# Moving a gate, a normalisation and a pair of rounded copies between the slots of a software-pipelined attention kernel

## The reference

```python
x = x + _L0_xattn_ref(_layernorm(x), ctx_2048, ...)   # banded attention, 8 heads, band 64
x = x + _L0_ffn_ref(_layernorm(x), ...)               # top half of the rows through a GELU network
x = x + _L1_xattn_ref(_layernorm(x), ctx, ctx, ...)   # grouped attention, 32 heads, 8 groups
x = x + _L1_ffn_ref(_layernorm(x), ...)               # squared-ReLU network, experts, normalisation
```

```python
x = jnp.transpose(mask, (0, 2, 1))            # mask: the normalised input, 64 x 256 for each of 16
qkv = x @ w_in.T + b_in
q, k, v = jnp.split(qkv, 3, axis=-1)          # 8 heads of 8
scores = jnp.einsum('bqhd,bkhd->bhqk', q, k) / jnp.sqrt(d)
scores = jnp.where(band[None, None], scores, neg)          # |q - k| <= 64
attn = jax.nn.softmax(scores, axis=-1)
o = jnp.einsum('bhqk,bkhd->bqhd', attn, v).reshape(n, t, e)
o = jnp.transpose(o @ w_out.T + b_out, (0, 2, 1))
y = jax.nn.relu(o) * encodings
out = jnp.einsum('nit,io->not', y, w_ct) + b_ct[None, :, None]
```

## Time and profile before

| | before |
|---|---|
| median of 3 runs | 334.32 us (333.77 to 334.48) |
| profiled execution | 333.68 us |
| its span | 331.9 us |
| mean granted TensorE clock | 0.997 |
| PE busy | 307.6 us (93%) |
| DVE busy | 238.3 us (72%) |
| ACT busy | 198.5 us (60%) |
| POOL busy | 181.1 us (55%) |

### The profile page before, as it was taken

How to read it: one execution, slowest core, us unless ns; L and a number is a source line. 1 busy time by engine, 2 the same in 40 slices (tenths; PEclk the granted TensorE clock), 3 DMA queues, 4 the chain that set the end, 5 groups by cost and what they waited for, 6 DMA issues and landing times.

```text
span 331.9 us, 7213 instructions
## 1 busy us (share of the span) xinstructions
PE 307.6 (93%) x2178; PEld 240.2 (72%) x2178; DVE 238.3 (72%) x919; ACT 198.5 (60%) x414; POOL 181.1 (55%) x294
## 2 busy tenths in 40 slices
PE   5997989999999999999998998989899999999993
PEld 4976667677777777776587876757677577898892
DVE  7878889999999999984426336875988647651354
ACT  3748987877778778777640424386878844114210
POOL 7738565677695947586613611453454942325522
PEclk9999999999999999999999999999999999999998
DMA  6999010201010110100000000000000000000000
GB/s 189 365 366 355 13 46 5 49 2 43 9 34 15 27 24 20 35 0 4 2 0 0 2 0 0 0 2 3 0 1 2 2 0 0 2 33 17 18 32 32
DMA packets 13301, 14.51 MB, mean 44 GB/s; under 512 B 2512, under 2 KB 11984, under 8 KB 13264
## 3 DMA queue, kind: packets, MB, share of 16 engines
q1 hardware_dynamic: 12688, 13.72, 13.2%
q10 hardware_dynamic: 576, 0.33, 0.3%
HBM read 10.64 MB, written 1.05 MB: 35 GB/s over the span
## 4 chain that ended last, share of the span: by engine, by line
PE 63%; POOL 12%; DVE 12%; issue 8%; ACT 4%; DMA 1%; POOLq 0%; SPq 0%; DVEq 0%; ACTq 0%
PE ST L803 8%; PE S L439 5%; PE O L466 5%; PE S L778 5%; PE ST L450 4%; PE S L573 4%; PE PJ L402 2%; POOL hT L1104 2%; POOL rstd L1088 2%; PE PJ L698 2%; PE S L721 2%; PE S L654 2%; DVE masked L1300 2%; POOL ex L1145 2%; DVE mw L1432 2%
## 5 line engine op out<-in xcount | busy, mean ns | idle before, releaser
L1300 DVE CUSTOM_DVE_ANT_0 masked<-S,band 128x192 bf16<-128x192 f32 x256 | 79.7, 353 | 9.0 <-PE S L439 7.3
L900 ACT ACTIVATE ex<-ST 128x384 f32<-128x384 f32 x128 | 60.8, 490 | 17.6 <-PE ST L450 16.1
L1085 POOL TENSOR_SCALAR rstd<-mv 128x1 f32<-128x1 f32 x40 | 12.0, 301 | 77.2 <-DVE mv L1236 76.9
L439 PE MATMUL S<-qk 128*128 128x384 f32 x128 | 52.2, 409 | 0.8 <-DVE mw L1300 0.4
L450 PE MATMUL ST<-qk 128*128 128x192 f32 x256 | 48.1, 271 | 2.4 <-ACT ex L900 2.0
L450 PEld LDWEIGHTS ST<-qk 128*128 128x128 f32 x256 | 45.0, 189 | 4.8 <-issue 4.2
L1145 POOL TENSOR_SCALAR_AFFINE_SELECT ex<-ex 128x512 f32<-128x512 f32 x32 | 20.3, 636 | 29.7 <-ACT ex L900 29.6
L466 PE MATMUL O<-ex,v 128*32 128x192 f32 x512 | 34.1, 338 | 0.0
L439 PEld LDWEIGHTS S<-qk 128*128 128x128 f32 x128 | 24.1, 189 | 13.3 <-issue 11.7
L869 ACT ACTIVATE hs<-PJ,sb,byhead 128x512 fp32r<-128x512 f32 x29 | 22.6, 778 | 11.1 <-PE PJ L403 10.8
L803 PE MATMUL ST<-down,hT 128*128 128x256 f32 x128 | 28.9, 379 | 0.0
(11 more groups left out here) (205 smaller groups left out, 717.6 us busy)
## 6 DMA issues: line engine op xcount, KB each, us to landing
qk<-kp SPq DMA_DIRECT2D x48, 48.0 KB
w<-in_w SPq DMA_DIRECT2D x2, 1024.0 KB, 10.1
cx<-in_cx SPq DMA_DIRECT2D x1, 1024.0 KB, 9.7
up<-in_up SPq DMA_DIRECT2D x1, 1024.0 KB, 11.7
down<-in_down SPq DMA_DIRECT2D x1, 1024.0 KB, 10.6
out<-x SPq DMA_DIRECT2D x8, 128.0 KB, 1.7
cxT<-in_cxT SPq DMA_DIRECT2D x1, 768.0 KB, 6.7
x<-in_x SPq DMA_DIRECT2D x1, 768.0 KB, 8.5
```

The costliest lines, as they stand in the source:

```text
L439: mm(out, r32(qp[:, t % 2, g, b, P * c:P * c + P]), r32(mv_), start=True, stop=True).then_inc(s["pe_s"], 1)
L900: A(ex[:, (n // 2) % 4, 2 * w:2 * w + 2, :], ST[n % 2][:, 0:2 * WIN].rearrange("p (h k) -> p h k", h=2), ACT.Exp, scale=SCALE).then_inc(s[ ...
L1300: last = V.tensor_tensor_reduce(out=masked[:, n % 2, h, :], in0=S[n % 2][:, WIN * h:WIN * h + WIN], in1=band[:, c, :], scale=1.0, scalar=N ...
```

## The change

The normalisation of tiles 2 to 7 moves from slot 9 to slot 11 on GpSimd, and behind the gate in the source. The gate moves from slot 11 to slot 10, where it stands before that slot's selects. For tiles 2 to 7 ACT's rounded copies move from slot 14 to slot 15, and VectorE's second low part from slot 1 to slot 0, right behind the first. No step is added or removed and no buffer or wait changes.

```diff
-        SLOT = {"stat": -25, "inv": -24, "norm": -23,
+        SLOT = {"stat": -25, "inv": -24, "norm": -21,
...
-                "turn": 39, "turned": 40, "weigh": 41, "relu": 42, "gate": 43, "gated": 45, "add": 46,
+                "turn": 39, "turned": 40, "weigh": 41, "relu": 42, "gate": 42, "gated": 45, "add": 46,
...
                 t = T_ + 2
-                if l == 14 and 0 <= t < TILES:
+                if l == (14 if t < 2 else 15) and 0 <= t < TILES:
                     act.wait_ge(*normalised(t))
...
-                t = due("norm", T_, l)
-                if t and t >= 2:
-                    pool.wait_ge(s["pool_rstd"], t + 1)
-                    pool.wait_ge(s["pe_v"], t - 1)
-                    normalise(xn[:, t % 2, :], t, "pool_xn")
                 t = due("gate", T_, l)
...
                     G.tensor_tensor(yr[:, 1, :], yr[:, 0, :], cx[:, t, :], ALU.mult).then_inc(s["pool_y"], 1)
+                t = due("norm", T_, l)
+                if t and t >= 2:
+                    pool.wait_ge(s["pool_rstd"], t + 1)
+                    pool.wait_ge(s["pe_v"], t - 1)
+                    normalise(xn[:, t % 2, :], t, "pool_xn")
...
-                if l == (2 if T_ < 1 else 1) and 0 <= t < TILES:
+                if l == (2 if T_ < 1 else 0) and 0 <= t < TILES:
                     dve.wait_ge(*rounded(t, 1))
                     V.tensor_tensor(r32(xs[0:64, 1, :]), xn[64:128, t % 2, :], xs[64:128, 1, :], ALU.subtract)\
```

## The result

| | before | after |
|---|---|---|
| median | 334.12 us (333.77 to 335.51, 6 runs) | 331.97 us (331.85 to 332.05, 6 runs) |
| profiled execution, its span | 333.68, 331.9 us | 331.85, 330.1 us |
| mean granted TensorE clock | 0.997 | 0.995 |

The ratio of after to before, run side by side, is 0.9932, with a 95% interval of 0.9916 to 0.9949: 2.2 us faster, 1.7 to 2.8. The forecast was 333.2, or 1.15 us faster, within 331.5 to 334.9.

The account below looks back on a forecast made before the run. VectorE was taken as nearly full (19.48 of 20.00 us), with two paths almost equal. Seams at 31, 48, 65 us and three later: -0.5 + 0.1 + 0 - 3 x 0.25 = -1.15; 334.32 - 1.15 = 333.2 us, range 331.5 to 334.9.

Parts of the forecast that it names:

- The seam's sum: From slot 13 of a tile to slot 3 of the next, VectorE gains 0.63 us if nothing is in the way.
- Gate 0.20: PE's gated product at slot 13 no longer waits for GpSimd's gate; VectorE can use 0.20 us of it.
- gap 0.15: VectorE's gap before the masked add of slot 1 goes, as S of slot 1 is early: 0.15 us.
- break 0.11: Back-to-back low parts leave VectorE three breaks between neighbouring operations instead of four: 0.11 us.
- slot 3 0.17: From the product of L1315 to the next operation VectorE takes 0.76 instead of 0.93 us: 0.17 us gained.
- the collision: In slot 0, VectorE's low parts and GpSimd's selects hold one another up, leaving 0 to 0.5 us of 0.63.
- A tie: First select and first low part both start at 84.24 us; the seam gains 0.51 or nothing, middle 0.25 us taken.
- Tiles 6 and 7 ... 0: These tiles have no copies and their gate already comes in time, so they gain 0.
- The seam at 31 us: PE's 0.60 us wait for the second low part mostly goes and PE carries it through the tile: -0.5 us.
- No collision: Rival: selects of slot 0 come wholly before or after the low parts; -3.0 us, 331.3 us, chance 0.20.
- kept port: Rival: GpSimd keeps the port over both selects of slot 0, delaying the first low part; +0.9, 335.2 us, chance 0.15.
- no effect: Rival: something counted as slack holds VectorE, or the 31 us stall moves elsewhere; within 0.3 us of before, chance 0.15.

Follow-up runs that it names:

- with the collision taken away: The changed kernel with GpSimd's selects of slot 0 at the six seams made to wait for the second low part: 330.0 us, 0.9884 of before.
- the last experiment: The changed kernel with the gates of tiles 4 and 5, which run beside tiles 6 and 7, back in slot 11: 332.36 us, 0.9954 of before.

## Why the prediction was half right

**The seam's sum held.** Gate 0.20, gap 0.15, break 0.11 and slot 3 0.17 made 0.63, and with the collision taken away the seams at 83, 101 and 119 us gave 0.62, 0.63 and 0.64. In that trace, at 83 us, the first low part starts 1.43 us sooner than before, 0.20 of it gained since the seam ahead, the masked adds of slot 1 start 0.04 us behind the end of the pair, and slot 3 takes 0.76 us. Alone, the gate gave 0.24 and the low part 0.27 (0.16 and its 0.11 of collision); the copies gave 0.10 alone and nothing within the whole at these seams, as long as the collision was there.

**"A tie" was none.** I had select and low part both begin at 84.24 us. In the trace the select is first, by 0.16 us, at every full seam. VectorE came 0.20 us sooner, as counted; PE did not come 0.31 sooner but 0.46 (its shift against before grows from -0.73 us at slot 6 to -1.19 at S of slot 14), and ACT and GpSimd with it. Half of that error is the product "without a wait": the one of 133.00 had itself waited, for a gate of the kernel before that ended at 132.95, 0.05 us ahead of it:

```profile
132.21 0.74 POOL L1122 TENSOR_TENSOR yr<-yr,cx 128x256 f32<-128x256 f32 x1
```

A start right behind the end of its input is no undisturbed start, whether or not the view prints a wait. Where the gate was long done, the product follows ST by 0.20 or 0.21 us (79.02, 131.62 and 147.02 us after the change), not 0.28. The other 0.07 us lies behind the product, in a piece that I had taken as unchanged: from its start to S of slot 14 PE takes 0.93 us (79.02 to 79.95) instead of 1.00 (80.14 to 81.14). Nothing on record says why. The other terms then follow by my own rule: with the select 0.16 us ahead the loss is 0.60 - 0.16 = 0.44, and the seam gives 0.63 - 0.44 = 0.19. I had taken the middle, 0.25; three seams give 0.59 instead of 0.75.

The rule of the Trainium skill, "SBUF — State Buffer", section "Who interferes with whom", that a VectorE operation with two SBUF inputs and a GpSimd one that reads SBUF exclude each other, agrees with the trace: when the two meet, the one that came second ends some 0.27 us (the low parts) or 0.50 us (the wide select) behind the end of the other, and the masked adds, which read their scores from PSUM and only the band from SBUF, take 0.35 us during a select.

**"Tiles 6 and 7 ... 0"** is the largest miss: -0.45, of which the last experiment takes 0.44 away. I had looked at slot 13 of tile 6 only, and read there a product that had waited. In tile 7 of the kernel before, the gate began behind two selects, ended at 148.64 us, and the product started right behind it:

```profile
147.91 0.73 POOL L1122 TENSOR_TENSOR yr<-yr,cx 128x256 f32<-128x256 f32 x1
```
```profile
148.70 0.70 PE L496 MATMUL XB<-yr,wc 128*128 128x256 f32 x2
```

The prediction called itself wrong if a gain arose outside the seams. A quarter of the gain did, so that in this it was wrong; the other sign, a period from 70 to 120 us outside 17.3 to 17.85, did not come (17.66). PE's projection without a wait, which it had also announced, holds at 31 us but not later.

**The seam at 31 us: nearly the right size, by luck, with the wrong mechanism.** -0.36 against -0.5. PE's wait for the second low part, which I had priced, is worth nothing by slot 6, since ACT is full there; the copies' move gave all of it (-0.37 alone, and -0.03 for the change without it), through ACT. The step that failed is "PE, which goes on without a gap from there, carries it through the tile": `hs` stands between.

**48 and 65 us:** -0.06 and -0.28 against +0.1 and 0; without the collision -0.43 and -0.65 against "about 0.3 each". The collision itself costs 0.37 at both. At 65 the missing 0.3 is for the most part the gate, which alone gave 0.22 there. At 48 the parts alone, with the low part's 0.11 of collision taken away, gave 0.28 and 0.11, together 0.39 of the 0.43; the prediction gives no terms for its 0.3, so which of them it had too small stays open.

In all: +0.14 at 31, -0.16 at 48, -0.28 at 65, +0.16 at the full seams and -0.45 behind them make -0.59, from -1.15 to -1.74. That errors of 0.30 one way stood against 0.89 the other is luck. That the medians differ by 2.15 us where the profiled executions differ by 1.83 lies within the interval. No collision was priced at -3.0 us and measured at -3.86, of which 0.54 lie behind the seams, where the price had nothing.

**The rivals.** The kept port and no effect are refuted. The collision is there, and it costs the change 1.9 us of span that the wait gives back.

## What to carry to other kernels

Before a step is moved into a slot, look at what the *other* engine of a shared port does there, and at which of them comes first: two gains on two paths of different size shift the tie that was computed for one. If the engine with slack can wait (here about 2 us before a select), one wait that serialises the pair can be cheaper than letting them meet: here it was worth 0.43 us at a seam where the select came first. (Where VectorE came first, with the second low part moved alone, the meeting took 0.11 us; the wait wasn't tried in that kernel.) Check a term of zero at each place to which the edit reaches, and take "undisturbed" from a place whose inputs were done well before.

## What the runs showed of the hardware

- Two engines that exclude each other alternate by operation, even between two selects issued back to back: 0.42, 0.52, 0.81 and 0.76 us for operations of 0.42, 0.42, 0.64 and 0.42.
- In a stretch of 1.7 us in which PE was busy 0.61 us its clock went to 1.2 GHz and stayed there for nearly seven microseconds, and in all 3.1 us were lost at this seam. In the changed kernel PE was busy 2.29 us of the 3.00 from 31 to 34 us and all of those from 33.0 to 34.7, and its clock stayed at 1.00.
